# Weighing two softmax steps together and moving the parts of a layer norm in an adaLN attention and mixture-of-experts block

## What is computed

```python
h = _layernorm(x) * (1 + ca) + sa
x = x + ga * attention(h)      # 16 heads, rotary, causal, softmax over 512 keys
h = _layernorm(x) * (1 + cb) + sb
x = x + gb * experts(h)        # t = slices of h @ Wm + bm, 8 per token
# experts: w = softmax(t @ emb); the two largest of 16; eo = gelu(t @ W1 + b1) @ W2 + b2
#          out = (sum of the two eo, weighted by w) @ Wo + bo
```

## Time and profile before

| | us |
|---|---|
| median of 3 runs | 380.09 |
| the profiled execution | 379.44 |
| its span, first to last instruction | 377.6 |
| PE busy | 337.4 |
| VectorE busy | 276.7 |
| ScalarE busy | 259.9 |
| GpSimd busy | 158.2 |

### The profile page before, as it was taken

The page is one execution under the profiler, slowest core; times in us unless marked ns, Lnnn a source line. Parts: engine busy times, 40 slices in busy tenths (PEclk is TensorE's granted clock), DMA queues, the critical chain, the costliest instruction groups (busy, mean ns, idle before and its releaser), DMA issues.

```text
span 377.6 us, 7238 instructions
## 1 busy us (share of the span) xinstructions
PE 337.4 (89%) x2656; PEld 154.0 (41%) x2656; DVE 276.7 (73%) x569; ACT 259.9 (69%) x282; POOL 158.2 (42%) x189
## 2 busy tenths in 40 slices
PE   5959688988899899799999899999998889789996
PEld 4524254645555434233654344435553313141123
DVE  5879968778899688779799676864589467953334
ACT  8680463445389888684488988855679797959980
POOL 6349299701407243852208054832140146232500
PEclk9987789999999999999999999999999999999999
DMA  7336131400027255500136255520060457625541
GB/s 266 116 66 82 27 63 42 57 5 3 3 51 97 73 139 155 170 23 0 32 77 85 77 137 138 145 48 8 26 86 0 123 137 137 120 67 138 152 133 30
DMA packets 27115, 31.46 MB, mean 83 GB/s; under 512 B 6780, under 2 KB 17788, under 8 KB 27068
## 3 DMA queue, kind: packets, MB, share of 16 engines
q1 hardware_dynamic: 23372, 28.50, 33.0%
q0 software_dynamic: 3456, 2.39, 3.1%
q10 hardware_dynamic: 252, 0.11, 0.2%
HBM read 3.50 MB, written 1.05 MB: 12 GB/s over the span
## 4 chain that ended last, share of the span: by engine, by line
PE 52%; DVE 24%; DMA 8%; issue 6%; ACT 5%; SPq 3%; POOL 1%; DVEq 0%; ACTq 0%; POOLq 0%
PE big L1360 18%; PE misc L1360 17%; PE acc L1360 16%; DVE mx L1080 7%; DMA dense<-tp 4%; ACT ring L818 3%; DMA gm<-wT 2%; PE misc L1395 2%; DMA block<-qk_turned 1%; SPq L501 1%; DVE gm L1207 1%; DVE second L1172 1%; DVE xn L1014 1%; SPq L526 1%; SPq L448 1%
## 5 line engine op out<-in xcount | busy, mean ns | idle before, releaser
L818 ACT ACTIVATE ring<-big 128x1024 f32<-128x1024 f32 (+1 forms) x201 | 195.3, 1022 | 72.2 <-PE big L1360 71.3
L1080 DVE TENSOR_REDUCE mx<-misc 128x1 f32<-128x512 f32 (+7 forms) x155 | 87.4, 588 | 27.0 <-PE misc L1360 25.1
L1360 PE MATMUL acc<-ring,cb 128*32 128x512 f32 x512 | 67.8, 604 | 3.1 <-ACT ring L818 1.6
L1360 PE MATMUL big<-tstack,w1s 128*128 128x512 bf16 x192 | 55.0, 381 | 4.2 <-ACT ring L818 3.8
L1360 PE MATMUL big<-dense,block 128*128 128x512 bf16 (+7 forms) x256 | 51.7, 307 | 0.9 <-DMA dense<-nm 0.5
L1360 PE MATMUL misc<-dense,block 128*128 128x320 bf16 (+7 forms) x170 | 43.8, 317 | 8.3 <-DVE mx L1080 7.9
L1207 DVE SCALAR_TENSOR_TENSOR gm<-acc,cb,gm 128x512 f32<-128x512 f32 (+1 forms) x41 | 30.0, 734 | 27.3 <-PE acc L1360 19.4
L455 POOL DMA_DIRECT2D block<-qk_turned x66 | 39.3, 600 | 2.5 <-DMA tstack<-tp 2.1
L1360 PEld LDWEIGHTS misc<-dense,block 128*128 128x128 bf16 x170 | 20.7, 150 | 47.0 <-DVE mx L1080 37.9
L700 POOL TENSOR_TENSOR gm<-osb,gm 128x512 f32<-128x512 f32 x12 | 15.8, 1317 | 57.4 <-ACT osb L867 42.7
L1360 PEld LDWEIGHTS big<-dense,block 128*128 128x128 bf16 x256 | 28.7, 149 | 24.5 <-ACT ring L818 9.7
(11 more groups left out here) (173 smaller groups left out, 476.8 us busy)
## 6 DMA issues: line engine op xcount, KB each, us to landing
gm<-wT SPq DMA_DIRECT2D x64, 256.0 KB
dense<-qk SPq DMA_DIRECT2D x42, 64.0 KB
tstack<-tp SPq DMA_DIRECT2D x18, 128.0 KB, 5.0
block<-qk_turned POOLq DMA_DIRECT2D x66, 32.0 KB, 3.3
xs<-in_x SPq DMA_DIRECT2D x4, 256.0 KB, 7.4
out<-lg SPq DMA_DIRECT2D x3, 256.0 KB, 2.5
dense<-tp SPq DMA_DIRECT2D x6, 128.0 KB, 9.9
dense<-nm SPq DMA_DIRECT2D x45, 4.0 KB, 1.8
```

What stands on the lines that cost most here:

```text
L818: act.activation(dst, src, func, scale=scale).then_inc(s["ring_read"], 1)
L1080: dve.tensor_reduce(mx[:, g, k:k + n, blk], src, AX.X, ALU.max).then_inc(s["misc_read"], 1)
L1360: return pe.matmul(dst, lhsT, rhs, start=start, stop=stop)
```

## The change

`softmax` and `slots` take two steps from `late` whenever three are waiting, where they took one. So steps 0 and 1 are weighed behind the scores of step 2, steps 2 and 3 behind those of step 4, 4 and 5 behind 6, 6 and 7 behind 8, and 8 and 9 at the end. Before, step k was weighed behind the scores of step k + 2, and steps 7, 8 and 9 at the end together. The odd steps are thus weighed one step of scores earlier. In the first stage the maxima stay between the weighings, and are dealt anew over the slots.

In the first experts stage the norm of batch 3 is dealt otherwise: statistics of tiles 2 and 3 behind n = 4 (was 5), variance behind 5 (was 7), root and tile 0 behind 11 (was 12), tiles 1 and 2 behind 13 (were 13 and 14), tile 3 behind 15 as before. POOL's power comes behind its product 7 (was 11).

```diff
@@ slots
             late.append(("weigh", g, i))
             if len(late) > 2:
-                order.append(late.pop(0))
+                order += [late.pop(0) for _ in range(2)]
@@ POOL, loops
-                experts_out(b, K_BLOCKS, {9: lambda: shift_rest(b + 2), 11: lambda: rsqrt(2 * b + 4, 0) if b + 3 < NB else None})
+                experts_out(b, K_BLOCKS, {7: lambda: rsqrt(2 * b + 4, 0) if b + 3 < NB else None, 9: lambda: shift_rest(b + 2)})
@@ DVE, norm_parts
-                return {3: first_tiles, 5: last_tiles, 7: lambda: variance(0, norm_link), 12: begin,
-                        13: lambda: normal(src, 0, 1), 14: lambda: normal(src, 0, 2),
-                        15: lambda: normal(src, 0, 3).then_inc(s["xn_ready"], 1)}
+                def middle():
+                    for t in (1, 2):
+                        normal(src, 0, t)
+
+                return {3: first_tiles, 4: last_tiles, 5: lambda: variance(0, norm_link), 11: begin,
+                        13: middle, 15: lambda: normal(src, 0, 3).then_inc(s["xn_ready"], 1)}
@@ PE, softmax
                         late.append((g, i))
                         if len(late) > 2:
-                            was = late.pop(0)
-                            weigh(m, phase, *was)
-                            if ("weigh", *was) in between:
-                                between["weigh", *was]()
+                            for was in [late.pop(0) for _ in range(2)]:
+                                weigh(m, phase, *was)
+                                if ("weigh", *was) in between:
+                                    between["weigh", *was]()
```

## The result

The changed kernel takes 383.07 us (median of 20 runs, 381.93 to 387.71), the kernel before beside it 380.18 (20 runs, 378.11 to 383.75): 0.8% slower, ratio 1.0082 with an interval of 1.0058 to 1.0107. The direction and its main cause were forecast; the size was not: 2.9 us in the medians and 2.6 us in the profiled executions (span 380.2 for 377.6), for a forecast of 5.55.

A forecast was written before the change was run, and what follows sets the result against it. PE and ACT hold each other through the two-unit `big`, and DVE's chain ends softmax stages with theirs. 1.9 + 1.9 + 2.45 + 0 - 0.7 = +5.55 on 379.44 gives 385.0, median 385.6 us; range 381.5 to 388.0.

The forecast's parts named there:

- the 0.13 us tail of a run: End of each run of weighings on PE: 0.13 us paid once per run, taken as the drain from changing tiling mode.
- The first exp of S7: Second softmax stage, ACT, score step 7 of S0 to S9: begins at about 116.35 us instead of 115.3, +1.0.
- the last exp of the stage: ACT, score step 9: second stage 122.65 us for 120.73, +1.9; fourth stage 285.9 for 283.41.
- ACT's wait ahead of S9: Sign in the changed trace: ACT's wait for `big` before score step 9's first unit grows to 1.5 us or more.
- A: Rival, chance 0.14: only DVE's chain gets longer; tokens cost +0.9, +0.9 and +0.8, norm -0.7, giving 382.0 us.
- B: Rival, chance 0.10: faster, if PE's own work is the bound; nine merges give 2.0 us, 377.4 with the norm's 0.7.
- C: Rival, chance 0.05: nothing changes; the moved weighings and the norm cancel, 380.1 us.
- D: Rival, chance 0.05: more is lost; the first stage also pays or a later stage has less cover, over 388 us.
- W5 and W7: Second stage, weighings of steps 5 and 7, each now ahead of scores for which ACT is idle: half of +1.9 each.
- the first stage at nothing: First softmax stage: 0, bounds -0.5 to +1.0 us, since ACT has slack of more than half the stage.
- Table load, first gelus, hidden units and the routing transpose follow that exp in order, so 126.04 becomes 127.95: End of second softmax stage: the last exp's delay reaches the routing transpose in full, +1.9 us in each of two stages.
- the norm: First experts stage: -1.9 for the old place, +0.4 variance, +0.8 root; net -0.7 us, bounds -1.9 and +0.5.

The follow-up runs named there:

- e3_w23: Kernel before with only the weighings of steps 2 and 3 paired, in stages 2 to 4: 382.4 us, ratio 1.0055 (8 runs).
- e5_w67: Kernel before with only the weighings of steps 6 and 7 paired, in stages 2 to 4: 380.13 us, ratio 1.0000 (8 runs).
- e4_w45: Kernel before with only the weighings of steps 4 and 5 paired, in stages 2 to 4: 381.95 us, ratio 1.0013 (8 runs).
- e6_w67_last: All pairs, norm as before, but in stages 2 to 4 weighings 6 and 7 go to the end with 8 and 9: 383.53 us, ratio 1.0107.
- e11_collision_back: `e8_norm_root12` with POOL's first two additions put behind its product 5, beside the variance's new place: 382.41 us, ratio 1.0075 (8 runs).
- e7_sums_early: Kernel before, norm and weighings unmoved, with POOL's first two additions behind its product 5 instead of 7: 384.17 us, ratio 1.0091 (10 runs).
- e1_pairs_only: Kernel before with the pairs of weighings in all four softmax stages, norm parts unmoved: 385.9 us, ratio 1.0130 (6 runs).
- e2_norm_only: Kernel before with the norm parts and POOL's power moved as in the change, single weighings: 378.45 us, ratio 0.9954 (12 runs).
- e8_norm_root12: `e2_norm_only` with the root and tile 0 left behind 12: 377.14 us, ratio 0.9897 (6 runs).
- e10_root12_weights_first: `e8_norm_root12` with DVE's copy of `wT` ahead of its copy of the second half's sums: 378.25 us, ratio 0.9943 (12 runs).

## Why the prediction was right in direction and too large

**Right: the mechanism and its places.** A pair takes 1.87 us. (That the 0.13 us tail of a run is the drain that the prediction took it for was not tested; only the saving was seen.) The first exp of S7 was forecast for 116.35 and came at 116.21, the last exp of the stage for 122.65 and came at 122.52, with the trace 0.28 us early as a whole; in the fourth stage 285.9 was forecast and 286.81 came, 0.75 of it carried in. ACT's wait ahead of S9 grew to 1.53 us, and `second` was ready 0.8 us before the transpose. Rivals A and B fell with that: `tf` is late by one weighing (+0.89) as A says, but the exps set the end, and nine merges that save PE's time (its busy time is 2.2 us less) bought nothing. C fell with the interval, and D since no later stage paid more. One sign of the forecast failed in part: ACT's wait ahead of the first unit of S7 was to be 1.5 us or more, and it was 0.65 in the second stage (1.80 in the fourth). There the delay came through the exps before it, and W3 has a share in it (0.50 us of the last exp in `e3_w23`) where the working spoke of W5 and W7 alone.

**Right: the first stage at nothing.** From the first weighing on PE to the transposes of `y` it is 42.57 us before and 42.36 after (96.99 - 54.42, 96.71 - 54.35); the three profiled kernels with pairs there have 42.31 to 42.36, the ten without 42.04 to 42.57.

**Wrong: "Table load, first gelus, hidden units and the routing transpose follow that exp in order, so 126.04 becomes 127.95".** The step took the first gelu to be bound by the exp. It was bound by PE, 0.40 us later than the table load allowed, behind three weighings of which the change takes one away. The idle time of 0.29 us ahead of it stood in the trace of before, three rows behind those that I quoted. The exp alone was +2.06 against my 1.9; with the slack taken off, the stage gave 1.62. This is 0.3 us in each of three stages, 0.9 of the 3.0 us that were missing, and `e5_w67` against `e4_w45` and `e6_w67_last` show it.

**Wrong in size: the norm.** Forecast -0.7, measured -1.36 alone. The variance at 5 was +0.29 for a forecast of 0.4, the place it left 2.01 for 1.9 (of this the collision 1.41; it was two held operations, 0.47 and 1.26 us, where the prediction read one), the root ahead of product 12 0.79 for 0.8. The missing term is the root's leaving of the place behind 12: 0.43 us, most likely a second collision, which stood in the trace of before as an operation of 1.13 us beside POOL's product. I had looked for collisions where the change goes to, and at one of the two places that it leaves.

**Missed: the experts stages.** About 0.3 to 0.4 us in each of two and 0.3 in the rest, 1.1 us together, taken as zero. Work that stands between a stage's late end and what waits for it has time to be done meanwhile, so a delay at the end is not handed on in full. Half of one such 0.3 us was reproduced by the order of two copies; the rest stays open.

The remaining 0.28 is the stretch before the second stage, within what it moves by itself. Three errors and this chance difference have the same sign and make 3.0 us. The other way, the runs' median lies 1.0 us above the profiled execution of 382.04, where I had taken 0.65 as before. The median, 383.07, lies in the range, but below the band given to the forecast itself (383.3 to 388.0). It is nearer to rival A's 382.0 than to the forecast's 385.6, though A's mechanism is not what set the ends of the stages. So the mechanism was right, and that the range holds the number owes something to the room left for A: in part that is luck.

## What to carry to other kernels

Where two engines hand each other a buffer of two places, putting two weighings together saves the entries and ends of runs (0.22 us a merge here) and costs up to a whole weighing (0.87 us) wherever the other engine runs dry (0.88, 0.81 and 0.40 us at the three places here); put them together only where the other has a full buffer ahead of it. When a chain is made later, ask at each link what it waited for before: whatever it already waited for on another engine is taken off the delay. And look at small DVE operations, at the place they leave as at the one they go to, for one that takes many times its own length beside a POOL instruction: here such places were worth 1.4 us and, as far as the rows say, 0.4 us, and one made on purpose 2.9 us, or 4.4 with the fall of the clock; a stage's three merges save 0.66.

## What the runs showed of the hardware

Four-element operations of DVE (0.16 us alone) took 0.47 to 1.26 us beside POOL's `tensor_tensor` of 128x512, three in one run of six (`e11_collision_back`), while bn_stats of 128 columns under the same additions kept its 0.28 us (`e7_sums_early`).

PE's granted clock fell to 0.50 behind waits of 4.48 us (`e7_sums_early`), 3.38 us (`e11_collision_back`) and 1.95 us (`e1_pairs_only`), for some 3 us in each, and stayed at 1.00 behind the same 1.94 us in the profile of the kernel before.

Whether that 1.94 us also spreads the times of the kernel before is not shown. Of its 79 executions that stood beside the experiments, 13 have a mean granted clock of 0.978 or less, with a median of 382.7 us for 380.1 in the others. Of the 30 of the three kernels without that wait and with single weighings (`e2_norm_only`, `e8_norm_root12`, `e10_root12_weights_first`) none has, and of the 20 of the changed kernel, which lacks the wait too, one has. But no trace of such an execution of the kernel before was taken, the 2.6 us are more than the 1.56 of one fall, and `e7_sums_early` has a fall in an execution with a mean of 0.982. So it is a likely reading at best.
